# Second attention of a two-layer language-model tower: masking in place on VectorE instead of mask products on TensorE

## The reference

```python
draft = jnp.einsum('bhqd,bhkd->bhqk', qr, kr)                 # 32 heads, 8 of keys
draft = draft + jnp.where(causal_future, neg, 0.0)
num_remain = max(min(Sq, MIN_REMAIN), Sq - int(Sq * MASK_OUT))   # 128
_, draft_indices = jax.lax.top_k(draft, num_remain)
mask = jnp.full((B, H, Sq, Sq), neg, dtype)
mask = mask.at[b_idx, h_idx, s_idx, draft_indices].set(0.0)
scores = jnp.einsum('bhqd,bhkd->bhqk', qr, kr) / np.sqrt(HD) + mask
attn = jax.nn.softmax(scores, axis=-1)
out = jnp.einsum('bhqk,bhkd->bhqd', attn, v)
```

## Time and profile before

| | |
|---|---|
| median of 3 runs | 4968.22 us (4965.84 to 4972.65) |
| the profiled execution | 4971.85 us, its span 4969.9 us |
| PE busy | 4028.0 us, 81% |
| DVE busy | 3258.2 us, 66% |
| ACT busy | 2802.1 us, 56% |
| POOL busy | 570.6 us, 11% |
| second attention | about 2165 to 4650 us of the span |

### The profile page before, as it was taken

How to read it: one execution, slowest core, us unless ns; L and a number is a source line. 1 busy time by engine, 2 the same in 40 slices (tenths; PEclk the granted TensorE clock), 3 DMA queues, 4 the chain that set the end, 5 groups by cost and what they waited for, 6 DMA issues and landing times. The chain is left out here.

```text
span 4969.9 us, 85458 instructions
## 1 busy us (share of the span) xinstructions
PE 4028.0 (81%) x25611; PEld 2331.5 (47%) x25752; DVE 3258.2 (66%) x9570; ACT 2802.1 (56%) x6546; POOL 570.6 (11%) x1877
## 2 busy tenths in 40 slices
PE   6998999999999989954777467766777777776899
PEld 2445766667444444422444234433444444443454
DVE  3555777777233345548877887887787888786244
ACT  1114777777000001147888588888888888887100
POOL 1000000000000000002122121221221221222000
PEclk8999999999999999976787677777877777777899
DMA  3326322222211113221111011111011111010542
GB/s 143 78 67 168 81 56 72 66 68 64 94 51 51 54 34 78 67 56 22 28 28 25 4 28 28 25 28 28 5 28 28 28 25 28 10 22 6 135 111 78
DMA packets 308441, 260.38 MB, mean 52 GB/s; under 512 B 188672, under 2 KB 242704, under 8 KB 307920
## 3 DMA queue, kind: packets, MB, share of 16 engines
q1 hardware_dynamic: 307376, 254.32, 20.1%
q0 software_dynamic: 544, 0.07, 0.0%
HBM read 176.21 MB, written 78.12 MB: 51 GB/s over the span
## 5 line engine op out<-in xcount | busy, mean ns | idle before, releaser
L1086 ACT ACTIVATE a_sign<-arena,a_state 128x384 fp8e4<-128x384 f32 (+5 forms) x1056 | 917.6, 870 | 88.6 <-DVE a_state L1259 50.2
L980 PE MATMUL a_ps_s<-k,q 128*128 128x512 bf16 (+3 forms) x1475 | 390.4, 397 | 401.5 <-DVE arena L1361 260.0
L992 PE MATMUL a_ps_t<-ident,arena 128*128 128x128 f32 x1584 | 343.6, 335 | 258.4 <-ACT a_probT L1054 244.4
L1054 ACT ACTIVATE a_probT<-a_ps_t 128x512 f32<-128x512 f32 (+3 forms) x768 | 363.9, 478 | 244.4 <-PE a_ps_t L999 238.9
L1086 ACT ACTIVATE a_sign<-a_third,a_state 128x384 fp8e4<-128x384 f32 (+2 forms) x480 | 417.2, 871 | 71.9 <-DVE a_state L1298 59.2
L738 ACT ACTIVATE a_prob<-a_x_neg,a_shift 128x640 f32<-128x640 f32 (+7 forms) x512 | 397.2, 776 | 90.0 <-DVE a_x_neg L781 63.4
L980 PEld LDWEIGHTS a_ps_s<-k,q 128*128 128x128 bf16 x1536 | 145.7, 115 | 560.9 <-DVE arena L1361 289.6
L781 DVE TENSOR_SCALAR_CACHE_REDUCE a_x_neg<-a_ps_s 128x640 f32<-128x640 f32 (+7 forms) x512 | 378.6, 751 | 41.9 <-PE a_ps_s L662 26.2
L677 PE MATMUL a_ps_t<-ident,a_prob 128*128 128x128 f32 x2304 | 365.0, 282 | 35.9 <-issue 16.3
L1309 DVE MAX8 a_nine<-a_below 128x8 f32<-128x256 f32 (+6 forms) x448 | 371.0, 828 | 34.4 <-issue 1.7
L1018 PE MATMUL a_ps_o<-a_probT,vals 128*64 128x128 f32 x4608 | 393.0, 316 | 0.0
(11 more groups left out here) (262 smaller groups left out, 7169.3 us busy)
## 6 DMA issues: line engine op xcount, KB each, us to landing
q<-qk SPq DMA_DIRECT2D x256, 256.0 KB, 4.6
qk<-p_qkT SPq DMA_DIRECT2D x32, 960.0 KB, 6.2
h_rows<-h SPq DMA_DIRECT2D x32, 512.0 KB, 6.8
k<-qk SPq DMA_DIRECT2D x256, 64.0 KB, 4.9
h<-tok_h SPq DMA_DIRECT2D x16, 512.0 KB, 4.0
arena<-in_wo SPq DMA_DIRECT2D x16, 512.0 KB, 6.4
o<-a_o SPq DMA_DIRECT2D x16, 512.0 KB, 2.7
q<-o SPq DMA_DIRECT2D x16, 512.0 KB, 5.5
```

Source lines behind the costliest of these rows:

```text
L980: nc.tensor.matmul(score(n)[:, a:a + w], q[:, y, head, i * P:(i + 1) * P], k[:, y, a:a + w], start=(y == 0), stop=False, skip_group_check= ...
L992: nc.tensor.matmul(to[:, c:c + P], xs[old][:, at:at + P], ident[:, :], start=(c == 0), stop=False, is_transpose=True, skip_group_check=True)
L1054: nc.scalar.activation(probT[:, n % 4, 0:w], ps_t[:, (n + 1) % 2, 0:w], ACT.Exp).then_inc(probT_ready, 1)
L1086: ins = nc.scalar.activation(to, xs[mine][:, at:at + w], ACT.Sign, scale=-1.0, saturate=False, bias=state[:, par, 0, n:n + 1], accum_out=s ...
```

## The change

VectorE's `fetch` multiplies the scores by 2^-13. `mark` no longer writes a mask: it writes (x < limit) - x over the scores themselves, so a kept score is -x and a masked one is 1 - x. ScalarE's Exp has a scale of -8192 (of +8192 for tile 0, which has no mask), so that a masked score comes to Exp at -8192 and gives 0. The mask products leave TensorE's turn, and the mask's buffer goes. GpSimd's split of the maxima works on `top` itself, without the negation, and `row_of` has a minus for tile 0.

The order of `mark` changes: twelve in pass 2 (ranks 0 to 11: all of the first head, tiles 1 to 5 of the second), two in pass 3, and no wait for TensorE between them. `exact_where_needed` moves to pass 3 and has no mark of its own; its copy of the tile takes the sign back. One semaphore step, `masked`, comes behind it in place of fourteen. TensorE waits for it ahead of the first turn, and for the last output only behind the second pair of turns. The copy of the output goes from VectorE's pass 3 to ScalarE, behind pass 4.

```diff
@@ TensorE, turn
-                        mm = nc.tensor.matmul(to.rearrange("p (b c) -> p b c", c=P), row_of[:, m * TT + i, :],
-                                              topT[:, :].unsqueeze(1).to_broadcast([SPLITS * 2 * TT, w // P, P]),
-                                              start=False, stop=(i == 0), skip_group_check=True)
-                        for c in range(0, w if i else 0, P):
-                            at = ps_seg(m, i) + a + c
-                            mm = nc.tensor.matmul(to[:, c:c + P], mask[:, at:at + P], ident_b[:, :], start=False,
-                                                  stop=True, skip_group_check=True)
-                        mm.then_inc(turn_done, 1)
+                        nc.tensor.matmul(to.rearrange("p (b c) -> p b c", c=P), row_of[:, m * TT + i, :],
+                                         topT[:, :].unsqueeze(1).to_broadcast([SPLITS * 2 * TT, w // P, P]),
+                                         start=False, stop=True, skip_group_check=True).then_inc(turn_done, 1)
@@ TensorE, value stage
-                        pe.wait_ge(mask_ready, (s - 2) * NS + NS)
-                        if not (isinstance(s, int) and s == 2):
-                            pe.wait_ge(o_ready, s - 2)
+                        pe.wait_ge(masked, s - 1)
                         for n in range(0, NC, 2):
...
                             turn(*CH[n + 1])
+                            if n == 2 and not (isinstance(s, int) and s == 2):
+                                pe.wait_ge(o_ready, s - 2)
@@ ScalarE
-                        nc.scalar.activation(probT[:, n % 4, 0:w], ps_t[:, (n + 1) % 2, 0:w], ACT.Exp).then_inc(probT_ready, 1)
+                        nc.scalar.activation(probT[:, n % 4, 0:w], ps_t[:, (n + 1) % 2, 0:w], ACT.Exp,
+                                             scale=(-1 if i else 1) / DOWN).then_inc(probT_ready, 1)
+
+                    def output():
+
+                        act.wait_ge(pv_done, (s - 2) * (NC // 2) + NC // 2)
+                        if not (isinstance(s, int) and s == 2):
+                            act.wait_ge(o_out, (s - 2) * 64)
+                        nc.scalar.copy(o[:, :], ps_o[:, :]).then_inc(o_ready, 1)
...
+                        if p == PASSES - 1 and st["value"]:
+                            output()
@@ VectorE, mark and fetch
-                        return nc.vector.tensor_scalar(mask[:, at:at + w], old_x[:, at:at + w], limit[:, r:r + 1], MASKED,
-                                                       ALU.is_lt, ALU.mult)
+                        nc.vector.scalar_tensor_tensor(out=old_x[:, at:at + w], in0=old_x[:, at:at + w],
+                                                       scalar=limit[:, r:r + 1], in1=old_x[:, at:at + w], op0=ALU.is_lt,
+                                                       op1=ALU.subtract)
...
-                        nc.vector.tensor_scalar(new_x[:, at:at + w], score(n)[:, 0:w], 1.0, None, ALU.mult, ALU.max,
+                        nc.vector.tensor_scalar(new_x[:, at:at + w], score(n)[:, 0:w], DOWN, None, ALU.mult, ALU.max,
@@ VectorE, order
-                    KEEPS = [n for n in range(NS) if RANKED[n][1] < HALF], [n for n in by_row if RANKED[n][1] >= HALF]
+                    KEEPS = range(0, NS - 2), (NS - 2, NS - 1)
...
-                            if st["keep"]:
-                                if st["value"]:
-                                    dve.wait_ge(turn_done, (s - 2) * TURNED + wide_turned)
-                                for r in KEEPS[1][0:2]:
-                                    mark(r).then_inc(mask_ready, 1)
-                                exact_where_needed()
                             dve.drain()
                         if p == 3:
                             if st["keep"]:
-                                for r in KEEPS[1][2:]:
-                                    mark(r).then_inc(mask_ready, 1)
+                                for r in KEEPS[1]:
+                                    mark(r)
+                                exact_where_needed()
+                                dve.sem_inc(masked, 1)
...
-                        if p == 3 and st["value"]:
-                            output()
```

More of the change, by code:

```diff
@@ L846, in kept_attention @@
     RANKS = TT - 1
+    DOWN = 2.0 ** -13
     with ExitStack() as ctx:
@@ L856, in kept_attention @@
         xs = (arena[:, 0:2 * SEG], arena[:, 2 * SEG:4 * SEG], third[:, :])
-        mask = sb("mask", [P, 2 * SEG], BF16)
         probT = sb("probT", [P, 4, BANK])
@@ L887, in kept_attention @@
         t_ready, signs_done = sem("t_ready"), sem("signs_done")
-        top_ready, mask_ready = sem("top_ready"), sem("mask_ready")
+        top_ready, masked = sem("top_ready"), sem("masked")
         ranked, chosen, told = sem("ranked"), sem("chosen"), sem("told")
@@ L893, in kept_attention @@
         EARLY = {16: range(0, 4), 20: range(4, NARROW)}
-        wide_turned = 2 + max(n for n, m, i, a, w in CH if i < HALF + 1)
         half_turned = 2 + max(n for n, m, i, a, w in CH if i < HALF)
@@ L1167, in split_top @@
                         wait_alone(pool, x_ready, (s + 2) * (2 * TT), const_in, 48)
-                        nc.gpsimd.tensor_scalar(neg[:, :], top[:, :], -1.0, 0.0, ALU.mult, ALU.add)
-                        pool.drain()
-                        nc.gpsimd.tensor_copy(top_b[:, 0, :], neg[:, :])
+                        nc.gpsimd.tensor_copy(top_b[:, 0, :], top[:, :])
                         pool.drain()
                         nc.gpsimd.tensor_copy(hi, top_b[:, 0, :])
-                        nc.gpsimd.tensor_tensor(rest[:, :], neg[:, :], top_b[:, 0, :], ALU.subtract)
+                        nc.gpsimd.tensor_tensor(rest[:, :], top[:, :], top_b[:, 0, :], ALU.subtract)
                         pool.drain()
@@ L1195, in _ @@
                 nc.vector.memset(code[:, :], 0.0)
-                nc.vector.memset(floor[:, :], MASKED)
+                nc.vector.memset(floor[:, :], -MASKED * DOWN)
                 nc.vector.memset(marked[:, :], 0.0)
@@ L1204, in _ @@
                 nc.vector.tensor_tensor(rows[:, :], rows[:, :], of[2], ALU.add)
+                dve.drain()
+                for m in range(2):
+                    only = rows[:, m * TT:m * TT + 1]
+                    nc.vector.tensor_scalar(only, only, -1.0, None, ALU.mult)
                 dve.drain()
@@ L1246, in start @@
                         dve.drain()
-                        nc.vector.scalar_tensor_tensor(out=var[:, :], in0=stats[:, :, 2], scalar=1e-20, in1=stats[:, :, 5],
+                        nc.vector.scalar_tensor_tensor(out=var[:, :], in0=stats[:, :, 2], scalar=1e-28, in1=stats[:, :, 5],
                                                        op0=ALU.add, op1=ALU.add)
@@ L1334, in select_exactly @@
                         left, lost = below[:, 0, 0:w], below[:, 1, 0:w].bitcast(I32)
-                        nc.vector.tensor_copy(left, old_x[:, at:at + w])
+                        nc.vector.tensor_scalar(left, old_x[:, at:at + w], -1.0, None, ALU.mult)
                         dve.drain()
@@ L1360, in fetch @@
                         dve.wait_ge(s_done, (s + 1) * (2 * TT) + (n + 1))
-                        nc.vector.tensor_scalar(new_x[:, at:at + w], score(n)[:, 0:w], 1.0, None, ALU.mult, ALU.max,
+                        nc.vector.tensor_scalar(new_x[:, at:at + w], score(n)[:, 0:w], DOWN, None, ALU.mult, ALU.max,
                                                 accum_out=top[:, m * TT + i:m * TT + i + 1]).then_inc(x_ready, 1)
-                    def output():
-                        dve.wait_ge(pv_done, (s - 2) * (NC // 2) + NC // 2)
-                        if not (isinstance(s, int) and s == 2):
-                            dve.wait_ge(o_out, (s - 2) * 64)
-                        nc.vector.tensor_copy(o[:, :], ps_o[:, :]).then_inc(o_ready, 1)
                     def scale_first():
@@ L1388, in exact_where_needed @@
                                     select_exactly(n)
-                                    if n in KEEPS[0] or n in KEEPS[1][0:2]:
-                                        mark(n)
                                 dve.nop()
```

2 lines of the change are left out of this document (removed).

## The result

The changed kernel takes 5037.0 us (4 runs, 5035.0 to 5042.8); the kernel before takes 4967.1 on the same chip (4 runs). The ratio is 1.014, with a 95% interval of 1.0123 to 1.0158. The predicted time was 4997 us, its range 4952 to 5033: the sign was right, the size was not.

A forecast was written before the change was run, and what follows sets the result against it. ScalarE's order of instructions was taken to set the period in the second attention. The terms, 60 - 32 - 4 + 3 + 4 - 2 = +29 us, gave a median of 4997 us, range 4952 to 5033.

The forecast's parts named there:

- values' load late: Every second slot's start: values wait for the later output copy, delaying ScalarE's first tile by 4.9 us; +60 us (42 to 77).
- mask products go: TensorE's turns end earlier without mask products, so ScalarE's Exps wait less: -32 us (-10 to -60).
- VectorE in passes 2 and 3, and the rest: Pass 2: -4 for the moved load and branch, +3 for longer marks; pass 3: +4; the last two slots: -2 us.
- costs the same 53 us: The one exact selection, moved from pass 2 to pass 3, keeps its price of 53 us.
- VectorE's 1.1 us of the earlier trace: Pass 0: from ScalarE's last Sign (T + 12.18) to VectorE's narrowing (T + 13.26); if all absorbed, the load costs 42 us.
- The sign that I named: ScalarE's waits for TensorE in places other than the late first Exps fall from 188 to about 155 us.
- shrinks to under 1 us but stays: VectorE's wait before the narrowing that ends pass 2, 3.88 us before in four of thirty slots, stays but under 1 us.
- VectorE becomes the bound: Rival: costlier marks make VectorE the bound of passes 2 and 3, each slot losing 1.3 us; +38, 5035 us; chance 0.15.
- By the sign that I gave: The page's slices of TensorE's granted clock stay at 7 with some 8; 6 and less means the clock rival is right.
- the clock rival: TensorE's clock stays at 1.2 GHz in passes 1 and 2, one more Exp a slot waits; +30, 5027 us; chance 0.10.

The follow-up runs named there:

- 4989.3: Changed kernel with the variance multiplied by 2^26 before the inverse square root and the two deviation tables by 2^-13: 4989.3 us.
- section 1: GpSimd tells that no row fails, so exact selections are left out: changed kernel 4929.8 us, kernel before 4915.0 us.
- section 4: Products of zeros put where the mask's were: added to the changed kernel 5089.7 us, added to the best version 4980.6 us.
- the kernel before with the early copy: Kernel before with the output copied by ScalarE behind pass 3, nothing else of the change: 4965.9 us.
- the best version: Changed kernel with the variance scaled back and ScalarE's copy of the output behind pass 3 instead of pass 4: 4940.2 us.
- the zeros: Products of a tile of zeros by the identity, as many as the mask's, added to the best version's turned tiles: 4980.6 us.
- The first run of section 3: Changed kernel with the copy of the output back on VectorE in pass 3: 5006.5 us.
- the runs of section 2: Changed kernel with: variance put back, 4989.3 us; factor 2^-12, 5040.6; no tie flag, 5034.7; no tie flag and rank rounded, 4993.0.

## Why the prediction was wrong, step by step

The measured +70 against the +29, by the runs:

| step of the prediction | predicted | measured |
|---|---|---|
| values' load late | +60 (42 to 77) | +49 (4989.3 - 4940.2); +48 in the kernel before |
| mask products go | -32 (-10 to -60) | -40 (32 to 40) |
| VectorE in passes 2 and 3, and the rest | +1 | +15 |
| exact selection "costs the same 53 us" | 0 | +48 (4989.3 to 5037.0) |

The third row is (4940.2 - 4965.9) + 40.4: the masking with its longer marks, without the products' gain, the load and the tie. The four add up to 72, where 70 were measured. They are good to some 5 us each: with all selections left out the first three come to 14.8 instead of 24. Part of that is the selection of slot 8, which costs 4989.3 - 4929.8 = 59.5 in the changed kernel by the medians, 7 more than before, and 2 more by the slots (section 1).

*The step that failed* is "the exact selection costs the same 53 us in pass 3 as in pass 2". As a price it holds within a few microseconds: 52 us in the kernel before, 56 for the same slot in pass 3. It was the number of selections that I took as given, though each is an event in the data, worth five times what a measurement can tell. The scaling by a power of two seemed to leave the search as it was. I didn't follow it through `start`, where one line treats a float's bits as a number. With this term the sum would have been 29 + 50 = 79 and the forecast 5047. With the variance put back, so that one selection is left, the change costs 4989.3 - 4964.5 = 25 us, where 29 were forecast.

*The values' load*: right in mechanism and place. The forecast said that nearly all of 4.9 us stays; narrowing came 4.1 us later (17.36 instead of 13.26; 3.8 to 4.7 in the eleven slots), in the three slots at the loop's back edge 0.9 to 1.2 (for example 17.88 instead of 16.67) where 2 was taken. 11 x 4.1 + 3 x 1.1 = 48, and 49 was measured. So VectorE's 1.1 us of the earlier trace rows, which I took as not absorbed and allowed for in the lower bound, was mostly absorbed. That the sum comes out so well is partly luck: between the two kernels that price the load, 4989.3 and 4940.2, slots 2 to 30 differ by 39.5 us in pass 0 and 18.6 in pass 1, and pass 2 takes 9.7 back. The issue 4 us into the slot, the first Exp's wait of some 5 and the copy's length (1.07 forecast, 0.99 seen) came as written.

*The mask products*: 32 forecast, 40 measured by the medians and 32.3 over slots 2 to 30 of the profiled executions. The sum is about right, its split was not: I had counted some 16 in pass 1 and 18 in pass 2, and 28.5 and 7.5 were seen (section 4). That the errors cancel is luck. The sign that I named, a sum of 155 us in the changed kernel's waits, can't be read there (184.2), since the late load's waits, 14 of about 5 us, fall in the same sum. In the version with the load hidden it is 149.9.

*VectorE*: I wrote that the wait before the narrowing that ends pass 2 "shrinks to under 1 us but stays", and that "issue" in most slots would mean that VectorE has become the bound. "issue" stands there in 18 of the loop's 24 slots, and pass 3 is hidden by a hair (0.15 us) where it is hidden. So the rival "VectorE becomes the bound" was right about who ends pass 2, and wrong about the price. The masking costs 15 us by the medians where the table has +1, but little of it lies in those passes. Between the kernel before with the early copy (4965.9) and the best version with the zeros (4980.6), which have the same work on TensorE, the profiled executions differ by 14.5 us: 4.7 ahead of slot 2, 5.3 in slot 8, whose selection stands in another pass, 3.4 behind slot 30, and 1.1 in the other 28 slots together (pass 2 is 9.1 longer, the other passes 8 shorter). As for the rival, its 5035 is near the measured time by accident, since it had neither the second selection nor the smaller stall. The first run of section 3 shows what was saved by taking the copy from VectorE: some 17 us net.

*The clock*: the slices went from 7 and 8 to 6 and 7. By the sign that I gave ("at 6 and less the clock rival is right") it would be half right; the runs of section 4 say that it isn't. A lower clock beside less work can come with a gain, as here; a price for the clock alone isn't in these runs.

## What to carry over

Ask of every changed number whether data-dependent work hangs on it, and count its events in the trace before and after: scaling by a power of two can leave a trace where a step reads a float's bits. The copy on the waiting engine was free here, but look who waits for a copy's end: behind pass 3 or behind pass 4 is 49 us here. To price a relief that is mixed with another wait, put the same work back as zeros in a version where the other wait is gone. Compare sums of waits over the same slots, never over the same stretch of time.

## What the runs showed that was not expected

By the runs of section 2, what VectorE makes of the bit pattern as a number differs by more than the power of two: the same scores give a tie in slot 15 with factors of 2^-12 and 2^-13, and none with 2^-6 or with the variance put back. The Trainium skill ("VectorE: DVE Perf Modes", Specifications) says that VectorE computes in float32 and that integers are exact only below 2^24. A float's bits as a number are far above that, so by this rule they would be rounded. The runs fit, but none reads the rounded value itself; that link is argued, not shown.

What stays open: why pass 1 of the kernel before takes 14.1 us in some slots and 16.4 in others (the same with zeros), and why the zeros cost more where the load is late. Neither was tried.
